# A Mamba block with a codebook FFN on one core: x dt, D x and half of the segment terms moved off GpSimd in two of its stages

## The chip, the cores and the metric

The kernel runs on one core of one Trainium2 chip. The metric is the device time of a launch in microseconds; the time before is the median of 3 runs. The engines are called PE (TensorE, matmuls), DVE (VectorE), ACT (ScalarE), POOL (GpSimd) and SP (SyncE, which here issues DMAs only).

## The reference, cut to what matters

```
x = x + layernorm(mamba(layernorm(x)))          # x: 4 x 1024 tokens of 512
x = x + layernorm(ffn(layernorm(x)))
mamba:  z, x, B, C, dt = split(u @ W_in.T)      # 512, 512, 64, 64, 8
        x, B, C = silu(conv4(x, B, C))          # causal, depthwise, 4 taps
        dt = softplus(dt + bias);  dA = exp(dt * A)          # 8 heads of 64
        S = S * dA_t + dt_t * outer(x_t, B_t)   # state 64 x 64 a head
        y = S @ C_t + D * x
        return (y * silu(z)) @ W_out.T
ffn:    w = lut[idx]                            # 16 levels, gate, up and down
        return (silu(x @ gate.T) * (x @ up.T)) @ down.T      # 512 -> 1376 -> 512
```

## The kernel before

The 4096 tokens are eight tiles of 512, a tile is four chunks of 128 tokens. A stage t runs the scan of tile t chunk by chunk, prepares tile t + 1 (projection, convolution, step sizes, z) and works on the FFN of tile t - 2 (LAG = 2). Two stages come without FFN work: tiles 0 and 1. In them the FFN weights are decoded, 20 half units a stage. For a half unit ACT turns codes into fp16 (L850), DVE makes 8 masks of 128 x 832 (L1524), PE adds them up with diagonals of the levels in two banks, 8 matmuls each (L1247), and ACT copies high and low halves out of the banks (L861, L862). Three banks turn. These stages are called decode stages here; stages 2 to 7 are FFN stages, and two tails follow.

The order of the work is written out by hand, one list an engine, with semaphores between them. A chunk c of the scan goes like this:

- POOL builds the segment terms (`segments`, L583 to L591): the causal 0/1 matrix times dt A of each of 8 heads, once for the fp16 high piece and once for the low piece, each one instruction of 128 x 1024. It may start when the inner products of the chunk before are done, since the terms lie in `decay`.
- PE turns x to token order (`prepare_x`, L1258), makes the Gram matrix of B and C and the sums (`prepare_small`), and multiplies the segment terms with a triangular matrix (`segment_sums`, L1285 to L1294), which waits for both pieces.
- ACT copies x out of its bank (L871), exponentiates the sums and the segments (`small`, `decays`); DVE multiplies by the Gram matrix (`decayed`).
- POOL (`weights`, L593 to L612) makes x dt (L598), x D (L602) and x dt times the remaining decay (L609).
- PE (`scan`, L1296 to L1314) makes the carried part of y in one bank, the inner part in another (eight fp32 products of 64 columns, L1308), and the addition to the state. POOL scales the state by its decay (L624).
- DVE (`y_sum`, `y_gated`, `y_split`) adds the two parts, updates the state (L1635), adds x D (L1640), multiplies by z and splits y into two fp16 pieces, between whose short steps it makes masks. SP transposes them by DMA for the output projection. DVE takes statistics of its result (L1663), POOL makes scale and bias of them in eight one-column instructions (L638, `out_rstd`), and ACT applies them (L895, `normalise`).

Before stage 0 the start loads and splits W_in, projects tile 0 and prepares its first chunk. There POOL makes both segment pieces of chunk 0 (L589) after the first scale of the second input pair (L580); PE waits at L1291 for them.

ACT's list in a decode stage mixes emptying decode banks (`decoded`), turning codes, the small copies above, the convolution's input, and the two normalisations; each engine's list is worked off strictly in order.

## Time and profile before

| | us |
|---|---|
| median of 3 runs (1386.94 to 1388.25) | 1387.95 |
| the profiled execution | 1389.47 |
| its span in the profile | 1387.3 |
| first scan to the last decoded unit | about 61 to 357 |

The profile is of one execution of this kernel. Its page gives busy time by engine and slice. Busy time of PE is modelled from pipelined matmuls and is no measure of how well the array is used. A wait is put down to the semaphore event that came last.

### The profile page before, as it was taken

Reading aid. Unit: us, or ns where it says so; the run is one execution under the profiler, and the core shown is the slowest. Engines: PE = TensorE matmul, PEld = TensorE weight load, DVE = VectorE, ACT = ScalarE, POOL = GpSimd, SP = SyncE. Lnnn points to the kernel's source line nnn. Section 1 sums busy time; section 2 is a strip of 40 time slices with the busy share of each in tenths; the row PEclk is TensorE's granted clock in tenths of the full one; section 3 lists DMA queues with packets and bytes.
Section 4 is the critical chain, followed back from the end, with each engine's and each line's share of the span. In section 5 each row is a group of like instructions: output and inputs, shape, how many; then the busy total and the mean of one; then the engine's idle time right before and its main releaser. Section 6 shows DMA issues by size and latency. Waiting matters only on the chain. (4 is left out here: it accounts for less than half of the span.)

```text
span 1387.3 us, 18643 instructions
## 1 busy us (share of the span) xinstructions
PE 1300.3 (94%) x6656; PEld 629.3 (45%) x6656; DVE 975.4 (70%) x1895; ACT 545.6 (39%) x986; POOL 532.6 (38%) x723
## 2 busy tenths in 40 slices
PE   4778898988899999999999999999999999999997
PEld 2334344544444444444444445444444444444443
DVE  7989988998578756875687668865886555544332
ACT  5466576756434233332334243423433223132120
POOL 1433354434434434435333534364345344400102
PEclk9899999989999999999999999999999999999999
DMA  5044235423331224023302330142213212401201
GB/s 170 25 111 112 73 98 117 113 73 78 84 54 31 69 76 84 24 54 107 84 24 61 99 92 23 34 126 62 54 31 88 51 45 45 107 31 31 77 0 53
DMA packets 132812, 96.16 MB, mean 69 GB/s; under 512 B 102000, under 2 KB 102000, under 8 KB 132720
## 3 DMA queue, kind: packets, MB, share of 16 engines
q1 hardware_dynamic: 124752, 78.74, 22.6%
q10 hardware_dynamic: 7968, 16.23, 4.4%
q8 instruction: 53, 0.87, 0.3%
q14 instruction: 39, 0.32, 0.1%
HBM read 54.05 MB, written 16.78 MB: 51 GB/s over the span
## 5 line engine op out<-in xcount | busy, mean ns | idle before, releaser
L1341 PE MATMUL bank<-fxt,ffn_hi 128*128 128x512 f16 (+1 forms) x1408 | 420.3, 380 | 10.0 <-DVE gact L1673 8.4
L1341 PE MATMUL bank<-fxt,ffn_lo 128*128 128x512 f16 (+1 forms) x704 | 267.3, 380 | 0.0
L1341 PEld LDWEIGHTS bank<-fxt,ffn_hi 128*128 128x128 f16 (+1 forms) x1408 | 139.9, 100 | 180.8 <-DVE gact L1673 11.3
L1247 PE MATMUL bank<-mask,diag 128*128 128x416 f16 x640 | 126.0, 350 | 20.0 <-ACT ffn_lo L862 11.5
L624 POOL TENSOR_TENSOR state<-state,ex 64x512 f32<-64x512 f32 x32 | 37.5, 1173 | 261.9 <-PE bank L1304 260.8
L1355 PE MATMUL bank<-ffn_hi,h_hi 128*128 128x512 f16 (+1 forms) x352 | 133.5, 379 | 0.0
L1355 PE MATMUL bank<-ffn_hi,h_lo 128*128 128x512 f16 (+1 forms) x352 | 133.3, 379 | 0.0
L1355 PE MATMUL bank<-ffn_lo,h_hi 128*128 128x512 f16 (+1 forms) x352 | 133.3, 379 | 0.0
L589 POOL TENSOR_TENSOR decay<-causal_h,da 128x1024 f16<-128x1024 f16 x64 | 122.4, 1933 | 22.1 <-PE bank L1308 17.1
L1524 DVE TENSOR_SCALAR mask<-codes_h 128x832 f16<-128x832 f16 x320 | 120.7, 436 | 5.0 <-PE bank L1247 4.6
L1673 DVE SCALAR_TENSOR_TENSOR gact<-gact,bank 128x512 f32<-128x512 f32 (+1 forms) x88 | 60.3, 685 | 86.2 <-ACT gact L901 85.3
L1552 DVE SCALAR_TENSOR_TENSOR xs<-cin,conv_w_sb,xs 128x512 f32<-128x512 f32 x114 | 108.1, 949 | 17.1 <-ACT xs L805 13.9
L901 ACT ACTIVATE gact<-bank,c_gate_half 128x512 f32<-128x512 f32 (+1 forms) x88 | 60.0, 681 | 146.7 <-PE bank L1341 144.9
L1341 PEld LDWEIGHTS bank<-fxt,ffn_lo 128*128 128x128 f16 (+1 forms) x704 | 70.7, 100 | 81.9 <-issue 0.8
L1215 PE MATMUL bank<-xt,win_hi 128*128 128x512 f16 x320 | 98.0, 389 | 4.1 <-DVE win_lo L1968 4.1
L1247 PEld LDWEIGHTS bank<-mask,diag 128*128 128x128 f16 x640 | 62.2, 101 | 86.5 <-issue 17.6
L1185 PE MATMUL bank<-win_hi,xt 128*128 128x512 f16 (+1 forms) x512 | 92.4, 275 | 3.1 <-DMA xt<-xsplit 3.1
L907 ACT ACTIVATE h_hi<-hf 128x512 f16<-128x512 f32 (+1 forms) x88 | 55.0, 625 | 83.8 <-DVE hf L1682 83.7
L1185 PE MATMUL bank<-wout_hi,yt 128*128 128x512 f16 x256 | 82.5, 384 | 5.8 <-issue 3.5
L1546 DVE TENSOR_TENSOR xsplit<-ut,xsplit 128x512 f16<-128x512 f32 x62 | 45.7, 745 | 59.8 <-ACT xsplit L776 59.6
L766 ACT ACTIVATE ut<-ut,shift,rstd 128x512 f32<-128x512 f32 x62 | 49.8, 803 | 93.1 <-POOL shift L580 92.9
L580 POOL TENSOR_TENSOR vare<-mv,eps_c 128x2 f32<-128x2 f32 x32 | 18.9, 590 | 167.4 <-DVE mv L1541 167.3
(186 smaller groups left out, 2240.5 us busy)
## 6 DMA issues: line engine op xcount, KB each, us to landing
codes_sb<-codes ACTq DMA_DIRECT2D x76, 208.0 KB, 3.5
ures<-u SPq DMA_DIRECT2D x32, 256.0 KB, 3.1
x_scratch<-x SPq DMA_DIRECT2D x32, 256.0 KB, 2.4
ut<-x_scratch SPq DMA_DIRECT2D x16, 512.0 KB, 4.3
xres<-x_scratch SPq DMA_DIRECT2D x32, 256.0 KB, 3.2
out<-dn SPq DMA_DIRECT2D x32, 256.0 KB, 2.0
ut<-u SPq DMA_DIRECT2D x15, 512.0 KB, 4.5
ffn_hi<-w_in_t SPq DMA_DIRECT2D x4, 580.0 KB, 8.6
```

The source lines that it names most:

```text
L589: seg_ready.inc(nc.gpsimd.tensor_tensor(segs[:, n], causal_h[:].unsqueeze(1).broadcast_to((P, HEADS, P)), da[:, t % HALVES, c, n, :].unsqu ...
L766: norm_steps.inc(nc.scalar.activation(buf[:, s, :], buf[:, s, :], ACT.Identity, bias=shift[:, no % 2, s:s + 1], scale=rstd[:, no % 2, s:s ...
L901: gtanh_ready.inc(nc.scalar.activation(gact[0:w, :], banks[FFN_BANKS[2 * m % 3]][0:w, :], ACT.Tanh, scale=c_gate_half[0:w, :]))
L907: hhi_ready.inc(nc.scalar.activation(h_hi[0:w, m, :], hf[0:w, :], ACT.Copy))
L1185: last = nc.tensor.matmul(out_ap, lhs, rhs, start=(k == 0), stop=(k == len(pairs) - 1))
L1215: last = nc.tensor.matmul(p.bank[:], w[:, k, cols], xt[:, :, half, k, :], start=(k == 0 and n == 0), stop=(k == KC - 1 and n == 2))
L1247: last = nc.tensor.matmul(p.bank[:, 0:COLS], diag[:, q].rearrange("p n m -> p (n m)"), mask[:, n, q, j * COLS:(j + 1) * COLS], start=(q == ...
L1341: last = nc.tensor.matmul(bank, wt[:, c0:c0 + w], fxt[:, :, half, k, :], start=(k == 0 and n == 0), stop=(k == KC - 1 and n == 2))
L1355: last = nc.tensor.matmul(banks[FFN_BANKS[turn % 3]][:], h[0:w, m, tok], wt[0:w, d0:d0 + D], start=(m == 0 and n == 0), stop=(m == MB - 1 ...
L1524: ins = nc.vector.tensor_scalar(mask[:, n, q, :], codes_h[:, count % CODE_SLOTS, :], float(2 * q), None, ALU.is_equal)
L1552: chain(conv_steps, i, CSTEPS * o + k, nc.vector.scalar_tensor_tensor(conv_sum(i, f), conv_in(i, o)[:, k:k + TILE], conv_w_sb[:, f, k:k + ...
L1673: ffn_turn.inc(nc.vector.scalar_tensor_tensor(gact[0:w, :], gact[0:w, :], 1.0, banks[FFN_BANKS[2 * m % 3]][0:w, :], ALU.add, ALU.mult))
```

## The change

In the decode stages (t < 2) alone:

- x dt is made by ACT straight out of the bank of transposed x: eight activations of 128 x 64 with dt of the head as the scale, in place of one copy (`small_x`).
- D x is made by PE: four fp32 products of x (not transposed) with diagonal matrices that hold D, 128 columns each, added up in the bank of the inner products, which follow in the same accumulation (`scan`). The four diagonals lie in the buffer `xd`; POOL builds them once, in two instructions of 64 x 512, ahead of the maximum of W_in. DVE's addition of `xd` is replaced by a semaphore increment (`y_gated`).
- The low pieces of the segment terms are made by ACT, eight scaled causal matrices of 128 x 128 a chunk (`segments_low`), with a copy of the low pieces in fp32 that DVE makes once a tile. POOL keeps the high piece.
- POOL keeps only the decay-weighted product (`weigh_x`). The lists of POOL and PE are written as a decode stage and an FFN stage each; their order is otherwise as before.

FFN stages keep the old way; the waits on `xtok_ready` and `xd_ready` count from tile 2, and the first `weights` of tile 2 waits for the last scan of tile 1 too.

```diff
 def segments(t, c):                                   # POOL
...
-    for n in range(2):
+    for n in range(1 if t < LAG else 2):
         seg_ready.inc(nc.gpsimd.tensor_tensor(segs[:, n], ...
+def weigh_x(t, c):
+    pool.wait_ge(sums_ready.sem, sums_ready.now(t, c + 1))
+    pool.wait_ge(xdt_ready.sem, xdt_ready.now(t, c + 1))
+    xw_ready.inc(nc.gpsimd.tensor_tensor(xtok, xdt, ex[:, 1, :] ..., ALU.mult))
 def weights(t, c):
-    pool.wait_ge(xtok_ready.sem, xtok_ready.now(t, c + 1))
+    pool.wait_ge(xtok_ready.sem, xtok_ready.now(t - LAG, c + 1))
+    if t == LAG and c == 0:
+        pool.wait_ge(y_done.sem, y_done.now(t - 1, SUB))
...
+pool.wait_ge(s_small, 64)                             # POOL, start
+for b in range(2):
+    rows = slice(b * NST, (b + 1) * NST)
+    nc.gpsimd.tensor_tensor(d_diag[rows], ident ..., d_sb ..., ALU.mult).then_inc(s_ddiag, 1)
+pool.wait_ge(s_ddiag, 2)
...
 def small_x(t, c):                                    # ACT
     act.wait_ge(xtok_done.sem, xtok_done.now(t, c + 1))
+    if t < LAG:
+        if t == 0 and c == 0:
+            act.wait_ge(dt_steps.sem, dt_steps.now(t, 21))
+        else:
+            act.wait_ge(y_done.sem, y_done.now(t, c))
+            act.wait_ge(xw_ready.sem, xw_ready.now(t, c))
+            if c == 0:
+                act.wait_ge(dt_steps.sem, dt_steps.now(t, 21))
+        for n in range(HEADS):
+            last = nc.scalar.activation(xdt[:, n * HD:(n + 1) * HD], tok_bank[:, n * HD:(n + 1) * HD],
+                                        ACT.Identity, scale=dt4[:, t % HALVES, c, n:n + 1])
+        xdt_ready.inc(last)
+        return
+def segments_low(t, c):
+    if t > 0 or c > 0:
+        act.wait_ge(y_done.sem, y_done.now(t, c))
+    if c == 0:
+        act.wait_ge(s_da_low, t + 1)
+    for n in range(HEADS):
+        last = nc.scalar.activation(segs[:, 1, n, :], causal_h[:], ACT.Identity,
+                                    scale=da_low[:, t, c, n:n + 1])
+    seg_ready.inc(last)
...
 def decode_stage(t):                                  # ACT
+    segments_low(t, 1)
     decoded(t, 0)
...
+    segments_low(t, 2)
     decoded(t, 5)
...
+    segments_low(t, 3)
     decoded(t, 10)
...
+    if t + 1 < LAG:
+        segments_low(t + 1, 0)
     decoded(t, 15)
...
     conv_input(0, 3)                                  # ACT, start
+    segments_low(0, 0)
     codes_to_half(0)
...
 def scan(t, c):                                       # PE
     yi_done.inc(nc.tensor.matmul(carried_bank[:], cs[h, tok], state[h, :], start=True, stop=True))
+    if dec:
+        if t == 0 and c == 0:
+            pe.wait_ge(s_ddiag, 2)
+        for k in range(KC):
+            nc.tensor.matmul(inner_bank[:, k * P:(k + 1) * P], xs[:, half, k, tok], d_diag[:, k, :],
+                             start=(k == 0), stop=False)
...
-                                xdt[:, n * HD:(n + 1) * HD], start=True, stop=True)
+                                xdt[:, n * HD:(n + 1) * HD], start=not dec, stop=not dec or n == HEADS - 1)
...
     dt_steps.inc(nc.vector.tensor_scalar(dt4[:, p], dt[:], 0.25, None, ALU.mult))   # DVE
+    if i < LAG:
+        nc.vector.tensor_copy(da_low[:, i], da[:, p, :, 1, :]).then_inc(s_da_low, 1)
...
 def y_gated(t, c):
-    dve.wait_ge(xd_ready.sem, xd_ready.now(t, c + 1))
-    y_step(t, c, 3, nc.vector.tensor_tensor(y[:], y[:], xd[:], ALU.add))
+    if t < LAG:
+        dve.sem_inc(y_steps.sem, 1)
+    else:
+        dve.wait_ge(xd_ready.sem, xd_ready.now(t - LAG, c + 1))
+        y_step(t, c, 3, nc.vector.tensor_tensor(y[:], y[:], xd[:], ALU.add))
```

## Rows read from the trace of the kernel before

**Rows 1.** The page's slices: busy tenths of PE, DVE in 40 slices.
```profile
PE   4778898988899999999999999999999999999997
DVE  7989988998578756875687668865886555544332
```

**Rows 2.** Busy time by stretch, then granted clock, DMA share, GB/s.
```profile
61.00:357.00 296.00, 253.20 (x1371) 129.10 (x1369) 258.84 (x577) 187.98 (x342) 122.69 (x139) 0.94 0.39 97
500.00:1387.00 887.00, 873.85 (x4378) 417.16 (x4375) 560.01 (x1027) 274.22 (x496) 329.92 (x457) 1.00 0.23 59
```

**Rows 3.** Waits of PE, 61 to 357 us: total, times, longest.
```profile
PE bank L1266 <- DVE state L1635: 12.2, 3, 6.4
PE bank L1247 <- ACT ffn_lo L862: 11.5, 10, 3.7
PE bank L1247 <- DVE mask L1524: 8.5, 8, 3.9
PE bank L1185 <- issue: 3.5, 1, 3.5
PE bank L1185 <- DMA xt<-xsplit: 3.1, 1, 3.1
PE bank L1185 <- DMA yt<-ysplit: 2.3, 1, 2.3
```

**Rows 4.** Waits of ACT, 61 to 357 us.
```profile
ACT x L895 <- POOL obias L638: 27.6, 4, 9.2
```

**Rows 5.** Groups of POOL, 61 to 357: count, busy us, mean ns, idle.
```profile
L589 POOL TENSOR_TENSOR decay<-causal_h,da 128x1024 f16<-128x1024 f16 x16 | 31.6, 1993 | 4.0 <-PE bank L1308 3.6 <-POOL state L624 0.2
L598 POOL TENSOR_TENSOR xdt<-xtok,dt 128x512 f32<-128x512 f32 x9 | 11.9, 1325 | 13.6 <-ACT xtok L871 13.6
L602 POOL TENSOR_TENSOR xd<-xtok,d_sb 128x512 f32<-128x512 f32 x9 | 11.7, 1298 | 0.0
```

**Rows 6.** Groups of DVE, 61 to 357 us.
```profile
L1524 DVE TENSOR_SCALAR mask<-codes_h 128x832 f16<-128x832 f16 x320 | 120.7, 436 | 5.0 <-PE bank L1247 4.6
L1640 DVE TENSOR_TENSOR y<-y,xd 128x512 f32<-128x512 f32 x8 | 9.1, 1132 | 0.0
```

**Rows 7.** Two DVE lines, whole span: duration ns min/median/max.
```profile
L1524 DVE TENSOR_SCALAR mask<-codes_h x320: 355/368/2062, 61.6 to 343.6; 128x832 f16<-128x832 f16 x160
L1640 DVE TENSOR_TENSOR y<-y,xd x32: 657/679/2265, 73.6 to 1185.2; 128x512 f32<-128x512 f32 x32
```

**Rows 8.** DVE in order of time: start us, us, what.
```profile
68.46 5.19 DVE L1524 TENSOR_SCALAR mask<-codes_h 128x832 f16<-128x832 f16 x8
95.68 2.38 DVE L1524 TENSOR_SCALAR mask<-codes_h 128x832 f16<-128x832 f16 x8
```

**Rows 9.** POOL in order of time, beside the first of them.
```profile
67.83 3.88 POOL L589 TENSOR_TENSOR decay<-causal_h,da 128x1024 f16<-128x1024 f16 x2
```

**Rows 10.** ACT in order of time, at the start.
```profile
29.35 0.27 ACT L818 ACTIVATE dtr<-bank,c_in 128x32 f32<-128x32 f32 x1
29.52 0.19 ACT L795 ACTIVATE cin<-zero_c 128x3 f32<-128x3 f32 x1
46.10 0.97 ACT L850 ACTIVATE codes_h<-codes_sb,pair_bias 128x832 f16<-128x832 int32 x1
46.98 0.61 ACT L813 ACTIVATE cin<-xs 128x512 f32<-128x512 f32 x1
```

**Rows 11.** Group of ACT, 61 to 357 us.
```profile
L871 ACT ACTIVATE xtok<-bank 128x512 f32<-128x512 f32 x9 | 5.3, 590 | 3.4 <-PE bank L1266 2.6 <-issue 0.5 <-ACT codes_h L850 0.2
```

**Rows 12.** PE in order of time, idle time before it in brackets.
```profile
55.36 1.89 PE L1291 MATMUL bank<-decay,below_h 128*128 128x512 f16 x4 [7.60 <-POOL decay L589]
100.36 2.00 PE L1308 MATMUL bank<-xdt,decay 128*128 128x64 f32 x16
116.00 0.48 PE L1276 MATMUL bank<-cs,bs 64*128 64x128 f32 x2
116.33 0.22 PE L1277 MATMUL bank<-ident,bs 64*128 64x64 f32 x1
```

More of the change, by code:

```diff
@@ L607, in weights @@
                     pool.wait_ge(xdt_ready.sem, xdt_ready.now(t, c + 1))
-                    pool.wait_ge(xd_ready.sem, xd_ready.now(t, c + 1))
+                    pool.wait_ge(xd_ready.sem, xd_ready.now(t - LAG, c + 1))
                     xw_ready.inc(nc.gpsimd.tensor_tensor(
@@ L654, in add_output, with decode_stage @@
                     res_ready.inc(nc.gpsimd.tensor_tensor(dn[:, c % 2, :], dn[:, c % 2, :], xres[:], ALU.add))
+                def decode_stage(t):
+                    decay_state(t, 0)
+                    segments(t, 1)
+                    if t >= 1:
+                        out_rstd(t - 1, 3)
+                        add_residual(t - 1, 3)
+                    weigh_x(t, 1)
+                    pair_rstd("u", t + 1, 1)
+                    decay_state(t, 1)
+                    segments(t, 2)
+                    out_rstd(t, 0)
+                    add_residual(t, 0)
+                    weigh_x(t, 2)
+                    if t >= 1:
+                        pair_rstd("x", t - 1, 0)
+                    decay_state(t, 2)
+                    segments(t, 3)
+                    out_rstd(t, 1)
+                    add_residual(t, 1)
+                    weigh_x(t, 3)
+                    decay_state(t, 3)
+                    segments(t + 1, 0)
+                    out_rstd(t, 2)
+                    add_residual(t, 2)
+                    if t + 1 < LAG:
+                        weigh_x(t + 1, 0)
+                    else:
+                        weights(t + 1, 0)
+                    if t >= 1:
+                        pair_rstd("x", t - 1, 1)
+                    pair_rstd("u", t + 2, 0)
                 def stage(t):
@@ L751, in _ @@
                 segments(0, 0)
-                weights(0, 0)
-                for t in range(TILES):
+                weigh_x(0, 0)
+                for t in range(LAG):
+                    decode_stage(t)
+                for t in range(LAG, TILES):
                     stage(t)
@@ L1357, in down, with decode_stage @@
                     down_done.inc(last)
+                def decode_stage(t):
+                    scan(t, 0)
+                    decode(t, 0)
+                    prepare(t, 1)
+                    segment_sums(t, 1)
+                    decode(t, 1)
+                    decode(t, 2)
+                    if t > 0:
+                        project_out(t, 0)
+                    decode(t, 3)
+                    decode(t, 4)
+                    if t == 0:
+                        project_out(t, 0)
+                    scan(t, 1)
+                    decode(t, 5)
+                    project_dt(t + 1)
+                    project_conv(t + 1, 4)
+                    prepare(t, 2)
+                    segment_sums(t, 2)
+                    decode(t, 6)
+                    project_conv(t + 1, 0)
+                    decode(t, 7)
+                    project_out(t, 1)
+                    decode(t, 8)
+                    decode(t, 9)
+                    scan(t, 2)
+                    decode(t, 10)
+                    project_conv(t + 1, 1)
+                    prepare(t, 3)
+                    segment_sums(t, 3)
+                    decode(t, 11)
+                    project_conv(t + 1, 2)
+                    project_conv(t + 1, 3)
+                    decode(t, 12)
+                    project_out(t, 2)
+                    decode(t, 13)
+                    decode(t, 14)
+                    scan(t, 3)
+                    decode(t, 15)
+                    project_z(t + 1, 0)
+                    prepare(t + 1, 0)
+                    segment_sums(t + 1, 0)
+                    decode(t, 16)
+                    decode(t, 17)
+                    project_z(t + 1, 1)
+                    project_out(t, 3)
+                    decode(t, 18)
+                    project_z(t + 1, 2)
+                    project_z(t + 1, 3)
+                    decode(t, 19)
@@ L1386, in stage @@
-                    if ffn:
-                        gate_up(g, 4)
+                    gate_up(g, 2)
+                    gate_up(g, 3)
+                    project_out(t, 0)
+                    gate_up(g, 4)
                     scan(t, 1)
-                    if dec:
-                        decode(t, 5)
                     if nxt:
@@ L1451, in stage @@
                         segment_sums(t + 1, 0)
[L1452 to L1457 removed]
+                    down(g, 2)
                     if nxt:
@@ L1460, in stage @@
                     project_out(t, 3)
-                    if dec:
-                        decode(t, 18)
-                    if ffn:
-                        down(g, 3)
+                    down(g, 3)
                     if nxt:
@@ L1467, in stage @@
                         project_z(t + 1, 3)
-                    if dec:
-                        decode(t, 19)
                 def tail(t):
@@ L1497, in _ @@
                 prepare_x(0, 0)
-                for t in range(TILES):
+                for t in range(LAG):
+                    decode_stage(t)
+                for t in range(LAG, TILES):
                     stage(t)
```

119 lines of the change are left out of this document (38 added, 81 removed).

## The prediction

> **What bounds the kernel now.** I read the page's slices first. They are not alike: from the eleventh slice on TensorE (PE) stands at nine tenths, before it at seven to nine, and in those same early slices VectorE (DVE) stands at eight or nine and later at five to eight [rows 1]. The table of stretches shows it in microseconds: from 500 us on PE is busy 874 of 887 us, while from 61 to 357 us, the two decode stages, it is busy 253 of 296 and DVE 259 of 296, at a mean granted clock of 0.94, so part of PE's 253 ran at the lower of the two levels (1.2 against 2.4 GHz) [rows 2]. So the FFN stages are bound by PE and the decode stages by DVE together with short round trips. The change touches the decode stages and the start only; the FFN stages I leave as they are.
>
> The waits of PE in 61 to 357 us say whom it waited for [rows 3]. On DVE end: the state update 12.2, the masks 8.5, the transposed y (which DVE splits) 2.3, the transposed input (DVE's split feeds that DMA too) 3.1, and 3.5 shown as issue; that last one stands at the first output projection of tile 0, whose wait in the code is for the low half of W_out, a DVE instruction in the queue behind the masks, so I count it with DVE. Together 29.6 us. On ScalarE (ACT) freeing a decode bank: 11.5 us. ACT itself sat 27.6 us in front of the output normalisation for eight small POOL instructions, which in turn follow DVE's statistics [rows 4]: most of ACT's idle time is DVE's lateness handed on.
>
> **Removed from POOL.** Per chunk of 128 tokens one of two segment products, the x times dt product and the D times x product. There are 8 chunks in the decode stages (the ninth instance in the window is tile 2's first chunk and stays): 8 x 1.99 = 15.9, 8 x 1.33 = 10.6 and 8 x 1.30 = 10.4 us, together 36.9 us [rows 5]. POOL has no share in the chain here, except through what it does to DVE.
>
> **Removed from DVE, directly.** y + xd, 8 times. Its median is 679 ns, its mean in the decode stages 1132 [rows 6, 7]. Undisturbed work: 8 x 0.68 = 5.4 us.
>
> **Removed from DVE, indirectly.** DVE slows while POOL works. Eight masks take 2.38 us in a quiet stretch and 5.19 us where the two segment products of 3.88 us lie beside them [rows 8, 9]: 2.81 us lost on 3.88, or 0.72 us for each us of POOL. That ratio is the upper end: 0.72 x 36.9 = 27 us. The lower end takes the masks alone: mean 436 ns against a median of 368 over 320 instructions is 22 us lost to all POOL work of the window, 122.7 us, or 0.18 per us, so 7 us [rows 2, 6, 7]. But masks are less than half of DVE's time, other two-input instructions show the same (y + xd gains 0.45 us each by this), and the three products removed are the long ones with large operands, whereas much of POOL's other time is one-column arithmetic. So I take a value near the upper row, 22 us, of which 3.6 belongs to y + xd itself. DVE falls by 5.4 + 22 = 27 us, with ends 12 and 32.
>
> A rule of the Trainium skill bears on this. "SBUF — State Buffer", section "Who interferes with whom", says that the two engines share one port pair as an exclusive lock: a VectorE instruction in a two-port mode or with two SBUF inputs and a reading GpSimd instruction do not share, one blocks wholly until the other ends. By that rule DVE would get back up to the whole length of each product beside which it has such work, up to 37 us; the trace has 0.72 on one overlap, with the direction of blocking decided by who came first. This is the larger-gain rival below. The same section says that ACT never waits for anyone, which no row here contradicts, so work moved to ACT should not be paid by DVE a second time.
>
> **Added to ACT.** Per chunk 16 small activations in place of one copy. Issue pace rather than duration counts. A 32-column one with a scale pointer from PSUM is followed by the next after 0.17 us; one of 832 columns after 0.88 us, though the duration is 0.97 [rows 10]. That is (0.88 - 0.17)/800 = 0.89 ns a column. So 128 columns: 0.17 + 96 x 0.00089 = 0.26 us, eight of them 2.0; 64 columns: 0.20 us, eight of them 1.6; less the copy of 0.59 [rows 11]. Net 3.0 us a chunk, 24 us in all, with ends 17 (the pace 0.17 for all sixteen) and 38 (durations instead of paces: 0.27 for 32 columns, so 0.30 and 0.36). ACT rises from 188 to 212 of 296 us.
>
> "ScalarE: Activation LUTs", section "Rules for kernel authors", in the Trainium skill, advises VectorE rather than ScalarE for a multiplication and budgets about 0.3 us an activation plus 0.83 ns an element. By that, called an estimate, the sixteen would cost 3.3 + 2.8 us, less the copy 5.5 a chunk and 44 in all; that rule is the one that speaks against this change.
>
> What of the 24 us lies on the path: the segment products stand where ACT otherwise waits for PE, just after the scan, before the first decoded half unit of the chunk is full (the state product and the eight matmuls of its first bank stand before that). ACT would be late there by perhaps 1 us. The x products stand in a stretch in which ACT empties banks while PE decodes, and delay each following bank by 1.0 us. PE has three banks and waited for ACT 11.5 us already. I put 2/3 us a chunk on PE's path, 5 us. Below lies 0 (hidden behind the waits of rows 4), above the whole 24.
>
> **Added to PE.** Four fp32 products of 128 columns a chunk, before the inner products. Nearest rows: one fp32 product of 128 columns stands as a pair (x2), 0.48 us with its tail, and by the starts the next instruction follows after 0.33 us; eight products of 64 columns (x16) 2.00 us, 0.25 each [rows 12]. So 4 x 0.25 = 1.0 to 4 x 0.33 = 1.3 a chunk, 8 to 10.5 us in all. The accumulation into the same bank changes nothing in the count of the inner products. They lie after the carried product and ahead of the waits for x dt and the decayed Gram matrix; PE waits for neither to speak of, so nothing hides them but PE's own idle time behind it. Where DVE sets the pace they are free, where PE does they cost in full. I take 8 us of 9.
>
> **Waits added.** ACT's segment products wait for the previous inner products, behind which PE must go anyway before it fills the next decode bank: no new lateness. The x products wait for POOL's weighing of the chunk before, long done. POOL's first full product for tile 2 waits for the last scan of tile 1, and stands behind the segments that wait for it already: nothing. DVE's replaced step is one semaphore increment. SP's queue keeps its order; its transposes come as DVE's splits do.
>
> **The start.** PE waited 7.60 us for the second segment product of chunk 0 [rows 12]; it now comes from ACT, whose input stands ready earlier, so PE goes on after one product instead of two: -1.95 us. x times dt by ACT is 1.6 us where copy and POOL product took 0.6 + 1.3 [rows 5, 11]: nearly even. The slow DVE work beside it gains about 0.5 more. The two new POOL products that build the diagonals fall into POOL's wait for the maximum of W_in; beside them DVE runs its reductions, and I put 0.5 us loss there. Sum -2.0, ends -4 and +1.
>
> **The sum in the decode stages.** Of PE's 29.6 us that end on DVE I let 22 go: DVE is 27 us lighter, but some waits then end on ACT or on DMA instead. With PE denser the clock drops less: 0.06 of 296 us is 18 us of lower granted clock, of which I take 3. So -22 - 3 + 8 + 5 = -12. The other account, from DVE: -27, less what DVE now waits more for ACT, PE and the code loads, gives -17 where the increase in waiting is 10. I take the middle, -14.5.
>
> With the start: -16.5. The profiled execution took 1389.47 us (span 1387.3); 1389.5 - 16.5 = 1373.0. The median is 1.5 us below that execution: 1371.5.
>
> **Rivals.**
> - *Larger gain.* DVE gets back almost all of the POOL time and PE follows: -28 to -32 from DVE. PE's own work is the floor: at the higher clock level and without a gap it would be 253 - 18 + 9 = 244 us against 296, so there is room. Gives about -28 with the start, 1360. For it: the 0.72 ratio, and that delays are passed round by ACT and POOL chains. Against it: ACT is then the next late one. Chance 0.16.
> - *Gain spent.* PE's 10 us and ACT's waits of 10 to 12 eat it; DVE's relief falls on stretches where it then waits for PE. Gives about -3, 1385. For it: DVE already waited for PE in places. Chance 0.14.
> - *Slower: ACT becomes the bound.* Place: the decode banks after a chunk's small copies. There ACT is already late: PE waited 11.5 us for it though ACT was busy only 188 of 296, so in a row of half units what ACT loses PE loses too. Price: the 38 us of the upper account in full, + 8 of PE, less everything that DVE held up (29.6, clock 3, start 2): +11, 1399. It decides from the point where a small activation costs its full duration and ACT's waits for the normalisation stay as long as now. The ScalarE page's budget of the Trainium skill would make it +17. Against it: 108 us of ACT idle time in the window, and those waits shrink with DVE. Chance 0.06.
> - *Forecast*, chance 0.64, its own spread 1364 to 1380.
>
> About 0.2%, 2.8 us, is what this measurement can tell from no change. Slower is the last rival's 0.06; half of "gain spent" lies within 0.2%, less what of it is beyond: 0.05; the rest 0.89 is faster. The range for 8 in 10 takes in part of the first rival and of the second: 1359 to 1382.
>
> **What would show it.** In the changed profile: the decode stages end near 340 instead of 357 us. The mask group keeps its count, with mean near 400 ns. DVE's busy time from the first scan to the end of decoding is 225 to 237 us. POOL's segment product occurs 8 times there. ACT's new groups show durations of about 0.30 and 0.36 us. PE's waits on DVE in the stretch are under 10 us, on ACT 12 to 18. PE's wait at the first segment sums is under 6 us. I would be wrong if masks kept their mean (the slowing comes then from the POOL work that stays), if PE's waits on ACT rose beyond 25 us, or if the time from 357 us on changed by more than 2 us.

## The result, and the profile after

| | before | after |
|---|---|---|
| median, 7 runs each on one chip | 1387.72 us (1386.68 to 1389.46) | 1382.71 us (1376.33 to 1383.88) |
| ratio, 95% interval | | 0.9946 (0.9931 to 0.9962) |
| profiled execution, its span | 1389.47, 1387.3 | 1382.02, 1380.3 |
| start: span's begin to the first scan | 61.9 | 66.7 |
| first scan to the ninth (the decode stages) | 291.6 | 279.1 |
| from there to the end | 1033.8 | 1034.5 |

The kernel is faster, as forecast, by 5 us between the medians and 7.5 us by the ratio (5.3 to 9.6), where 16.5 was forecast; 1382.71 lies just above the range, 1359 to 1382. The last three rows say where. I cut both spans at the carried product (PE's product of `state` and `cs`, L1304 before, L1390 after) of tile 0's first chunk, and at that of tile 2's, the ninth chunk. The decode stages got 12.5 us shorter, of 14.5 forecast. The start *grew* by 4.8 where it should have shrunk by 2.0. The spans differ by 7.0 where 16.5 was forecast; of the 9.5 us between, 6.8 are the start's, 2.0 the decode stages' and 0.7 lie behind them.

The two stretches as the view of stretches has them, first after (start, decode stages), then before, cut at the same points. Columns: length; busy us of PE, PEld, DVE, ACT, POOL with their instructions; granted clock; DMA share; GB/s.
```profile
0.00:66.70 66.70, 34.81 (x206) 17.16 (x206) 51.58 (x104) 34.93 (x61) 15.73 (x37) 0.95 0.29 89
66.70:345.80 279.10, 252.79 (x1409) 133.38 (x1408) 231.40 (x568) 212.42 (x452) 83.36 (x116) 0.95 0.41 101
```
```profile
0.00:61.90 61.90, 34.83 (x205) 17.11 (x205) 52.35 (x105) 32.45 (x53) 15.40 (x36) 0.92 0.31 96
61.90:353.50 291.60, 248.80 (x1346) 126.22 (x1345) 257.62 (x574) 186.96 (x340) 122.69 (x139) 0.94 0.39 97
```

In the decode stages DVE fell by 26.2 us, ACT rose by 25.5, POOL fell by 39.3, and PE rose by 4.0 though it got 9.3 us more work (below), at a granted clock that is 0.01 higher. The page's slices answer [rows 1]: PE's first one fell from 4 to 2 (the start), its fourth and fifth rose from 8 to 9, and of DVE's first ten three are 9 where five were. (On rows 1 the prediction says that PE stands at nine tenths from the eleventh slice; it is from the twelfth.)
```profile
PE   2879998988899999999999999999999999999997
DVE  6978977897678657875687558765886565544342
```

PE's waits in the decode stages, and ACT's largest, to be held against [rows 3, 4] (total, times, longest):
```profile
PE bank L1351 <- DVE state L1731: 9.0, 3, 4.0
PE bank L1332 <- ACT ffn_lo L917: 7.4, 4, 4.2
PE bank L1376 <- ACT decay L955: 3.5, 1, 3.5
PE bank L1270 <- issue: 2.8, 1, 2.8
PE bank L1332 <- DVE mask L1618: 1.8, 3, 1.1
PE bank L1270 <- DMA xt<-xsplit: 1.8, 1, 1.8
ACT x L974 <- POOL obias L656: 21.4, 4, 7.5
```
And the groups that the change touches, against [rows 5, 6] (count, busy us, mean ns, idle before it):
```profile
L1618 DVE TENSOR_SCALAR mask<-codes_h 128x832 f16<-128x832 f16 x320 | 109.5, 402 | 6.5 <-PE bank L1332 6.0
L596 POOL TENSOR_TENSOR decay<-causal_h,da 128x1024 f16<-128x1024 f16 x9 | 17.3, 1927 | 9.1 <-PE bank L1400 7.8 <-issue 1.1
L955 ACT ACTIVATE decay<-causal_h,da_low 128x128 f16<-128x128 f16 x56 | 17.1, 388 | 2.9 <-PE bank L1400 1.8 <-ACT codes_h L905 1.0
L935 ACT ACTIVATE xdt<-bank,dt 128x64 f32<-128x64 f32 x64 | 13.9, 324 | 2.4 <-PE bank L1351 2.2
L1395 PE MATMUL bank<-xd,xs 128*128 128x128 f32 x64 | 9.3, 288 | 0.0
```

The masks' mean went from 436 to 402 ns, POOL makes its segment product nine times in the stretch (seven, and both pieces of tile 2's first chunk; I had said 8) where there were sixteen, and the state wait fell from 12.2 to 9.0. One row is new: PE waited once, 3.5 us, for L955, the low segment pieces that the change gives to ACT.

### The profile page after: what moved, and what is told of

It is laid out like the page before. It is cut to its first block and busy times, and to the rows that moved or that the text cites. A ratio compares the mean times of both kernels' runs of the same rounds, so it can differ in the third digit from the quotient of the medians.

```text
span 1380.3 us, 18867 instructions
## 1 busy us (share of the span) xinstructions
PE 1305.2 (95%) x6720; PEld 636.7 (46%) x6720; DVE 949.3 (69%) x1889; ACT 573.5 (42%) x1106; POOL 494.7 (36%) x701
## 5 line engine op out<-in xcount | busy, mean ns | idle before, releaser
L1773 DVE SCALAR_TENSOR_TENSOR gact<-gact,bank 128x512 f32<-128x512 f32 (+1 forms) x88 | 60.2, 685 | 87.1 <-ACT gact L980 86.2
L1646 DVE SCALAR_TENSOR_TENSOR xs<-cin,conv_w_sb,xs 128x512 f32<-128x512 f32 x114 | 104.9, 920 | 19.9 <-ACT xs L860 16.8
L596 POOL TENSOR_TENSOR decay<-causal_h,da 128x1024 f16<-128x1024 f16 x56 | 105.8, 1908 | 27.2 <-PE bank L1400 21.3
L1618 DVE TENSOR_SCALAR mask<-codes_h 128x832 f16<-128x832 f16 x320 | 109.5, 402 | 6.5 <-PE bank L1332 6.0
L1332 PEld LDWEIGHTS bank<-mask,diag 128*128 128x128 f16 x640 | 62.6, 100 | 72.4 <-issue 14.4
L1640 DVE TENSOR_TENSOR xsplit<-ut,xsplit 128x512 f16<-128x512 f32 x62 | 43.5, 709 | 60.9 <-ACT xsplit L831 60.6
L1782 DVE SCALAR_TENSOR_TENSOR hf<-gact,bank 128x512 f32<-128x512 f32 (+1 forms) x88 | 60.3, 686 | 28.7 <-PE bank L1433 21.8
```

What stands on the lines that cost most here:

```text
L596: seg_ready.inc(nc.gpsimd.tensor_tensor(segs[:, n], causal_h[:].unsqueeze(1).broadcast_to((P, HEADS, P)), da[:, t % HALVES, c, n, :].unsqu ...
L1332: last = nc.tensor.matmul(p.bank[:, 0:COLS], diag[:, q].rearrange("p n m -> p (n m)"), mask[:, n, q, j * COLS:(j + 1) * COLS], start=(q == ...
L1618: ins = nc.vector.tensor_scalar(mask[:, n, q, :], codes_h[:, count % CODE_SLOTS, :], float(2 * q), None, ALU.is_equal)
L1646: chain(conv_steps, i, CSTEPS * o + k, nc.vector.scalar_tensor_tensor(conv_sum(i, f), conv_in(i, o)[:, k:k + TILE], conv_w_sb[:, f, k:k + ...
L1773: ffn_turn.inc(nc.vector.scalar_tensor_tensor(gact[0:w, :], gact[0:w, :], 1.0, banks[FFN_BANKS[2 * m % 3]][0:w, :], ALU.add, ALU.mult))
L1782: ffn_turn.inc(nc.vector.scalar_tensor_tensor(hf[0:w, :], gact[0:w, :], HSCALE, banks[FFN_BANKS[(2 * m + 1) % 3]][0:w, :], ALU.mult, ALU.m ...
```

## Where the start lost its gain

POOL in order of time, after (start, duration, what, idle time before it and what ended it):
```profile
17.61 2.72 POOL L789 TENSOR_TENSOR xd<-ident,d_sb 64x512 f32<-64x512 f32 x2 [5.84 <-DMA conv_w_sb<-conv_w]
26.04 0.38 POOL L795 PARTITION_ALL_REDUCE big<-lowest  x1 [5.71 <-issue]
36.88 0.35 POOL L797 PARTITION_ALL_REDUCE big<-lowest  x1 [10.46 <-DVE lowest L2121]
44.13 2.43 POOL L799 TENSOR_TENSOR diag<-fold,lut_sel 128x1024 f16<-128x1024 f32 x1 [6.90 <-issue]
```
The same two instructions of before, the first all-reduce and the first product behind the second:
```profile
18.60 0.38 POOL L742 PARTITION_ALL_REDUCE big<-lowest  x1 [6.81 <-DVE lowest L2004]
37.46 2.38 POOL L746 TENSOR_TENSOR diag<-fold,lut_sel 128x1024 f16<-128x1024 f32 x1 [7.47 <-issue]
```
The first all-reduce forms the maximum of W_in over partitions. Its input `lowest` is ready at 18.35 us in both kernels (DVE's reduction at 18.20 lasts 0.15). Before, it ran at 18.60. After, POOL's two diagonal products run from 17.61 to 20.33, and the all-reduce follows at **26.04**, not at 20.4: 5.71 us of "issue", in which POOL waited for nothing that is shown. The all-reduce's line in the view of one line, the sequencer's row of it, tells what lies in between. The last two times are those of its first and last occurrence. After, and then before:
```profile
L795 POOLq MODIFY_POOL_CONFIG  x2: 7/7/7, 20.3 to 20.3; - x2
```
```profile
L742 POOLq MODIFY_POOL_CONFIG  x2: 7/7/7, 11.7 to 11.8; - x2
```
A reconfiguration is put ahead of the all-reduce; I call it and what follows it a turn. Before, POOL had nothing to do from 11.79 us on, so it came at 11.8, and the 6.81 us of idle time that the row puts down to DVE's `lowest` hid it. Now it can only come behind the products, at 20.3, and is paid in full. A price for such a turn was in the trace of before: it stands on the way back from the second all-reduce to the next product, 7.47 us of "issue" (6.90 after), which I read past. There too the sequencer reconfigures, right behind the all-reduce (before):
```profile
L746 POOLq MODIFY_POOL_CONFIG  x2: 83/83/83, 29.9 to 30.0; - x2
```

The Trainium skill has the rule, "GPSIMD Engine Reference", section "2.1 Instruction dispatch": the first call to a freshly loaded kernel pays a load of about 6 us (5.95 measured, between MODIFY_POOL_CONFIG and the first instruction behind it, less the wait for events), without an instruction in the profile. The 5.71 us here agree, and the prediction did not weigh it. No run here shows what the engine does in that time.

PE's first projection and its first segment sums, after; then the first projection before:
```profile
30.78 1.01 PE L1300 MATMUL bank<-xt,win_hi 128*128 128x512 f16 x2 [11.34 <-DVE win_lo L2068]
60.47 1.04 PE L1376 MATMUL bank<-decay,below_h 128*128 128x512 f16 x2 [5.17 <-POOL decay L596]
```
```profile
23.54 1.01 PE L1215 MATMUL bank<-xt,win_hi 128*128 128x512 f16 x2 [4.07 <-DVE win_lo L1968]
```
W_in's scale hangs on the maximum, so PE starts 7.2 us later (30.78 against 23.54). Of these the start keeps 4.8; PE's wait at the segment sums fell from 7.60 [rows 12] to 5.17 us, 2.4 less, which is the gain that the prediction had seen there (1.95).

## The experiments

The ratios are against the kernel before, which ran beside each group of kernels (medians there 1387.76 to 1390.17), five rounds each; the row of before is that of the change's own comparison. "First scan" and "stretch" are cut as above, from the profiled executions; busy times are those of the stretch.

| kernel | median | ratio (95%) | first scan | stretch | DVE / ACT / POOL busy |
|---|---|---|---|---|---|
| before | 1387.72 | 1 | 61.9 | 291.6 | 257.6 / 187.0 / 122.7 |
| the change | 1382.71 | 0.9946 (0.9931 to 0.9962) | 66.7 | 279.1 | 231.4 / 212.4 / 83.4 |
| e1_diag_late | 1376.80 | 0.9914 (0.9891 to 0.9937) | 61.6 | 279.9 | 229.6 / 212.2 / 84.7 |
| e2_d_own_sem | 1376.50 | 0.9908 (0.9885 to 0.9930) | 62.4 | 277.6 | 230.2 / 212.9 / 81.2 |
| e3_before_diag_early | 1396.89 | 1.0051 (1.0035 to 1.0067) | 68.9 | 294.3 | 259.4 / 187.3 / 122.5 |
| e4_late_swap | 1377.42 | 0.9913 (0.9897 to 0.9929) | 61.8 | 282.2 | 230.6 / 212.9 / 86.8 |
| p4_d_only | 1381.67 | 0.9956 (0.9942 to 0.9971) | 64.2 | 283.3 | 246.8 / 187.1 / 106.9 |
| p1_no_seg | 1380.16 | 0.9939 (0.9917 to 0.9961) | 64.5 | 280.3 | 240.3 / 196.0 / 95.2 |
| p3_no_xdt | 1375.35 | 0.9900 (0.9882 to 0.9918) | 61.4 | 280.0 | 240.4 / 204.1 / 95.2 |
| c_no_d_pe | 1373.73 | 0.9878 (0.9856 to 0.9899) | 59.7 | 280.4 | 233.0 / 211.9 / 87.1 |
| c_pool_more | 1383.11 | 0.9957 (0.9941 to 0.9972) | 62.7 | 286.8 | 241.1 / 212.5 / 96.4 |
| c_act_twice | 1378.34 | 0.9935 (0.9914 to 0.9956) | 61.6 | 284.1 | 232.8 / 229.2 / 82.3 |
| **e5_diag_act** | **1372.68** | **0.9896 (0.9873 to 0.9918)** | 60.9 | 277.4 | 230.7 / 212.3 / 81.4 |
| b1_diag_act_no_xdt | 1375.66 | 0.9913 (0.9899 to 0.9927) | 59.4 | 282.7 | 239.4 / 203.6 / 93.9 |

First scan and stretch are of one execution each, so their spread matters. Five kernels share the change's decode stages (the change, e1, e2, e4, e5). Their stretches are 277.4 to 282.2 us; in them PE is busy for 250.8 to 254.9 us, at granted clocks of 0.94 to 0.96, and idle for 26.3 to 29.0. The kernel before and e3 share theirs: 291.6 and 294.3. c_no_d_pe has e1's code up to the first scan and comes to it at 59.7, e1 at 61.6. So under 5 us between two stretches, or 2 us between two first scans, can be no more than this spread.

### The start: e1, e2, e3, e4

**e1_diag_late** moves the diagonals behind both all-reduces.
```diff
-pool.wait_ge(s_small, 64); <two products>; pool.wait_ge(s_ddiag, 2)
 pool.wait_ge(s_lowest, 1)
 nc.gpsimd.partition_all_reduce(big[:, 0:1], lowest[:, 0:1], ...)
 pool.wait_ge(s_wbig, 1)
 nc.gpsimd.partition_all_reduce(big[:, 1:2], lowest[:, 1:2], ...)
+pool.wait_ge(s_wall, 1); <two products>; pool.wait_ge(s_ddiag, 2)
```


> The changed kernel with the two products that build the D diagonals moved behind POOL's two all-reduces, with a wait for the second of them. Theory A (turning POOL from elementwise products to an all-reduce costs it about 5.7 us after the last product, which the kernel before hid in its wait for the maximum of W_in and the changed kernel does not): the first all-reduce is back from 26.0 us to about 18.6, the first scan from 66.7 to about 59.3, and the time falls by 7.4 us from 1382.7 to about 1375.3. Theory B (only the lateness of the products themselves counts, 20.3 us against the 18.4 at which the maximum is ready, and the gap behind them is something of that execution): 1.9 us, about 1380.8.

**e2_d_own_sem** leaves them early but lets them wait for the load of D alone; the shared semaphore also waits for `conv_w`, which lands last.
```diff
-pool.wait_ge(s_small, 64)
+pool.wait_ge(s_dload, 16)
```


> The changed kernel with the diagonals where it has them, but waiting for the transfer of D alone (landed at 12.1 us) and not for all four small ones (the convolution weights land at 17.5). Theory A: products from 12.1 to about 14.5 us, the turn of 5.7 us until 20.3, so the first all-reduce at about 20.3 instead of 26.0: 5.7 us better than the changed kernel, about 1377.0, and 1.7 us behind the kernel with the diagonals late. Theory B: the all-reduce at 18.6, the same time as with the diagonals late.

**e3_before_diag_early** is the kernel before with the two products put in the same place, their result unused.
```diff
+pool.wait_ge(s_small, 64); <two products>; pool.wait_ge(s_ddiag, 2)
 pool.wait_ge(s_lowest, 1)
```


> The kernel before with the two products that build the diagonals added at the place the change gives them, with its wait; nothing uses them. Theory A: first all-reduce at 26.0 us, the time rises by 7.4 us from 1387.7 to about 1395.1, which is the whole of what the change lost at the start. Theory B: by 1.9 us, about 1389.6.

POOL of e1 and, behind it, DVE of e1; then POOL of e2; then POOL and PE of e3:
```profile
18.52 0.38 POOL L787 PARTITION_ALL_REDUCE big<-lowest  x1 [6.81 <-DVE lowest L2105]
37.05 2.83 POOL L794 TENSOR_TENSOR xd<-ident,d_sb 64x512 f32<-64x512 f32 x2 [7.15 <-issue]
37.56 1.42 DVE L1661 SCALAR_TENSOR_TENSOR cs<-cin,x 64x512 f32<-64x512 f32 x1
39.01 1.42 DVE L1656 SCALAR_TENSOR_TENSOR xs<-cin,xs 128x512 f32<-128x512 f32 x1
40.36 1.91 DVE L1676 TENSOR_SCALAR dtp<-dte 128x32 f32<-128x32 f32 x1
```
```profile
12.17 2.49 POOL L790 TENSOR_TENSOR xd<-ident,d_sb 64x512 f32<-64x512 f32 x2 [0.41 <-DMA d_sb<-d_param]
20.21 0.38 POOL L796 PARTITION_ALL_REDUCE big<-lowest  x1 [5.55 <-issue]
```
```profile
17.60 2.67 POOL L747 TENSOR_TENSOR xd<-ident,d_sb 64x512 f32<-64x512 f32 x2 [5.91 <-DMA conv_w_sb<-conv_w]
25.90 0.38 POOL L753 PARTITION_ALL_REDUCE big<-lowest  x1 [5.63 <-issue]
30.65 0.58 PE L1226 MATMUL bank<-xt,win_hi 128*128 128x512 f16 x1 [11.27 <-DVE win_lo L1979]
```

The reduction comes where the turn puts it: at 18.52 with no product ahead of it; at 20.21 where the products end at 14.66, that is 5.55 behind them; at 25.90 where they end at 20.27 (5.63 behind). In e3 nothing else is changed, and the kernel before gets 7.1 us slower by the ratio (4.9 to 9.3), its first scan comes 7.0 later, and PE's first projection stands at 30.65 as it does in the changed kernel. Seen against e3, the changed kernel's first scan is 2.2 us earlier: the gain of 2.0 that I had worked out for the start exists, under a cost of 7. So the turn behind the early products is shown as the cause: e3 adds it alone, e2 and e1 take it away. The rival that the expectations set against it, that only the 1.9 us count by which the products end too late, falls by e3, and by e2, where they end long before the maximum is ready. (By the ratios e2's interval lies clear of the change's; e1's overlaps it by a little.)

The recovery in e1 is 5.1 us of first scan against the changed kernel, and not the 7.4 expected. A part of the rest is seen: the products now lie at 37.05 to 39.88 beside DVE's convolution, whose two rows of e1 took 1.42 us each, where the kernel before has 0.69. The 1.91 us of the third row are not theirs; it took as long before, beside the level table's product alone:
```profile
37.97 1.91 DVE L1581 TENSOR_SCALAR dtp<-dte 128x32 f32<-128x32 f32 x1
```
DVE's step sizes, which the segment products need, come later by this, and PE's wait there is 6.74 us in e1 (5.17 in the changed kernel):
```profile
55.54 1.89 PE L1377 MATMUL bank<-decay,below_h 128*128 128x512 f16 x4 [6.74 <-POOL decay L596]
```

**e4_late_swap** is e1 with POOL's segment product of chunk 0 ahead of its scales for the second input pair.
```diff
-pair_rstd("u", 1, 0)
 segments(0, 0)
+pair_rstd("u", 1, 0)
```


> The kernel with the diagonals late, and POOL's high segment product of chunk 0 ahead of the scale of the second tile's first pair, for which PE had waited 5.2 us. By the timeline of the changed kernel, less 7.4 us, PE's wait at the first segment sums falls from 5.2 to about 1 us; but the x of chunk 0 is complete on DVE only 1.2 to 2.8 us before PE wants it now, so the first scan comes 1 to 3 us earlier: 1372 to 1374.5. If that wait is worth its whole length, 1371; if DVE sets the first scan, 1375.3 as without the swap.

PE in order of time:
```profile
51.20 1.04 PE L1377 MATMUL bank<-decay,below_h 128*128 128x512 f16 x4 [1.80 <-ACT decay L956]
60.76 1.12 PE L1352 MATMUL bank<-ident,xs 128*128 128x128 f32 x4 [3.34 <-DVE xs L1656]
```
PE's wait at the segment sums, 6.74 in e1, went down to 1.80, and the first scan did not move (61.8 against 61.6), where 1 to 3 us were expected: PE only waits 3.34 us later for DVE's convolution of x. That is the next late thing at the start; I had gone by the longest wait. (In this run alone the all-reduce came 7.87 us after the reconfiguration, at 19.61, which is 1.1 later than in e1 and can hide as much of a gain. I can't say why.)

### The parts: p4, p1, p3

All three are e1 with a part given back to POOL. **p4_d_only** gives back both x dt and the low segment pieces, so only D x on PE is left of the change; **p1_no_seg** gives back the segment pieces, **p3_no_xdt** x dt.
```diff
 def segments(t, c):                                # p1, p4
-    for n in range(1 if t < LAG else 2):
+    for n in range(2):
 def weigh_x(t, c):                                 # p3, p4
+    pool.wait_ge(xtok_ready.sem, xtok_ready.now(t, c + 1))
+    xdt_ready.inc(nc.gpsimd.tensor_tensor(xdt, xtok, dt4[...], ALU.mult))
```


> Of the change only the D products on PE (diagonals late), with x dt and both segment pieces on POOL as before. Theory C (moving the low pieces and x dt to ACT brings nothing between the scans, since each alone undone left the stretch at 280 us): stretch 279 to 282 us against 291.6 of the kernel before, first scan at about 64.5, ratio 0.992 to 0.994; the D part, 5.4 us of DVE and 10 of POOL, is then the whole gain of 12. Theory D (the two parts stand in for each other: each alone relieves POOL enough, both undone don't): stretch 285 to 289, ratio 0.996 to 0.999.

> The kernel with the diagonals late, and both segment products on POOL again (x dt stays on ACT, D x on PE). Base: 0.9914 of the kernel before, 279.9 us from the first to the ninth scan. Port theory (what counts is that POOL's long products slow DVE): 16 us of POOL come back, DVE loses some 0.6 of it, 10 us, of which half to two thirds show: the stretch is 5 to 7 us longer, the start 2 us more, ratio about 0.997. ACT theory (ACT's 19 us for the low pieces cost as much as POOL's relief brings): stretch the same or shorter, ratio 0.989 to 0.992.

> The kernel with the diagonals late, and x dt on POOL again from ACT's one copy (low segment pieces stay on ACT, D x on PE). Port theory: 10.6 us of POOL come back, DVE loses about 6, 3 to 4 show, less the 8 us of ACT time saved, of which 1 to 2 show: stretch 1 to 3 us longer, ratio 0.9925 to 0.994. ACT theory: the x products lie where ACT is late for PE's banks, so the stretch is 2 us or more shorter, ratio under 0.991.

The stretch of p4_d_only, and of e1 for comparison (columns as above):
```profile
64.20:347.50 283.30, 252.22 (x1409) 133.48 (x1408) 246.75 (x567) 187.11 (x340) 106.89 (x131) 0.96 0.39 100
```
```profile
61.60:341.50 279.90, 250.90 (x1409) 133.67 (x1408) 229.58 (x568) 212.21 (x452) 84.72 (x116) 0.95 0.39 101
```
D x on PE alone brings 8.3 of the 11.7 us that the stretch of e1 gains. The 25.1 us of work moved to ACT bring the other 3.4 (1.1 to 5.9 against the five stretches above), though they free DVE of 17.2 us. DVE's relief in the two steps is 10.8 and 17.2 us, and even at the ends of that spread the time follows the first far better than the second. p4's 283.3 and its ratio lie between the ranges of the two theories; by the ratios it is 5.8 us slower than e1, the intervals apart, of which 2.6 are the first scan's. Given back alone, either of ACT's parts changes the stretch by less than 0.5 us, with 11 us more on DVE and 8 to 16 less on ACT: neither of the theories set against each other for p1 and p3 came out whole. A gain from x dt on ACT is not seen: p3 is at 0.9900 against e1's 0.9914, the intervals overlap. The segment pieces seem to bring something at the start: without them the first scan comes 2.9 us later (64.5; 64.2 in p4), where both pieces of chunk 0 are POOL's again. The ratio of p1 overlaps with e1's.

Where ACT's side is paid shows in DVE's wait for `gram`, which ACT copies out behind the new activations. After the change, then p3, then p1:
```profile
DVE gram L1705 <- ACT gram L946: 7.9, 6, 3.8
```
```profile
DVE gram L1701 <- ACT gram L942: 1.8, 2, 0.9
```
```profile
DVE gram L1700 <- ACT gram L947: 5.5, 5, 2.1
```
It was 1.3 us before. In all three kernels without x dt on ACT (p3, p4, b1) it is 1.8; in e1, from which p1 and p3 are made, it is 8.1.

### The sizes: c_no_d_pe, c_pool_more, c_act_twice

**c_no_d_pe** leaves D x out of the decode stages altogether (part of the computation is missing), to price PE's products.
```diff
-for k in range(KC):
-    nc.tensor.matmul(inner_bank[:, k * P:(k + 1) * P], xs[...], d_diag[:, k, :], ...)
```


> The kernel with the diagonals late, without PE's D products in the decode stages: D x is left out there, so its time is that of the work without it. Eight times four products take 9.3 us of PE in the changed kernel's profile. If PE sets the pace of the decode stages now, as the prediction's term of 8 us has it: stretch 8 us shorter, ratio about 0.9855. If DVE still sets it most of the time: 0 to 3 us, ratio 0.989 to 0.9914.

By the medians they cost about 3 us of their 9.3, by the ratios 5, and the intervals overlap; the profiled stretch is not shorter at all (280.4 against 279.9), and that execution was the slowest of its kernel. Both values lie below the 8 that I charged, but the intervals leave anything from about 1 to 9, so this does not settle it.

**c_pool_more** makes the high segment piece twice on POOL, seven more products; **c_act_twice** makes the low pieces twice on ACT.
```diff
+nc.gpsimd.tensor_tensor(segs[:, 0], causal_h ..., da ..., ALU.mult).then_inc(s_extra, 1)
+pool.wait_ge(s_extra, t * SUB + c + 1)
```
```diff
-for n in range(HEADS):
+for twice in range(2): for n in range(HEADS):
     nc.scalar.activation(segs[:, 1, n, :], causal_h[:], ACT.Identity, scale=da_low[...])
```


> The kernel with the diagonals late, and in the decode stages POOL makes the high segment piece twice, the second time over the first. No other engine's work changes; the terms come 2 us later. Port theory: POOL has 15.5 us more of the kind that was taken away; masks and two-input instructions of DVE lengthen by about 10 us in sum, the stretch by 5 to 7 us plus 2 us at the start, ratio 0.9965 to 0.998. If POOL's time does not matter to DVE's pace: only the start's 2 us, ratio about 0.993.

> The kernel with the diagonals late, and ACT makes the eight low segment pieces twice, the second time over the first: 19.5 us more of ACT in eight places, nothing else changed. The prediction's term (24 us of ACT work put 5 on the path) gives +4 in the stretch and +2 at the start, ratio about 0.996. By the pair of kernels measured since (POOL's 15.5 us more cost 6.9 in the stretch, and the same with ACT's 19 us taken off cost 0.4), ACT's load is worth 6 to 7 in the stretch, ratio 0.997 to 0.999. If ACT's pieces are hidden in its wait for PE, stretch unchanged.

The stretch of each, with the wait of PE that grew:
```profile
62.70:349.50 286.80, 252.24 (x1410) 133.59 (x1409) 241.06 (x568) 212.47 (x452) 96.39 (x123) 0.95 0.40 98
PE bank L1358 <- DVE state L1738: 12.3, 3, 5.5
```
```profile
61.60:345.70 284.10, 254.16 (x1410) 134.19 (x1409) 232.83 (x569) 229.17 (x508) 82.28 (x116) 0.94 0.40 99
PE bank L1382 <- ACT decay L958: 5.6, 1, 5.6
```
13.5 us of POOL products (7 of 1923 ns) made DVE 11.5 us busier, 0.85 for each us, and the stretch 6.9 us longer, with PE idle for 34.6 us in place of 29.0. PE's wait for DVE's state update is 12.3; it is 8.2 to 9.1 in the five kernels above. By the ratios c_pool_more is 6.0 us slower than e1, the intervals apart. So POOL's products reach the time through DVE, with about 0.6 us of stretch for each us of DVE.

c_act_twice says less. 17.0 us of ACT came with a stretch 4.2 us longer, but PE's idle time grew by 0.9 of it only (29.0 to 29.9): its wait at the segment sums went from 3.1 to 5.6, and its wait for ACT's decode banks fell from 12.4 to 9.6. The other 3.3 us are PE's busy time, 254.2 against 250.9, for the same matmuls at a granted clock of 0.94 against 0.95; e4, with e1's decode stages, has 254.9 at 0.94. By the ratios it is 2.9 us slower than e1 and the intervals overlap. ACT's extra work costs at most about 0.25 for each us here; that it costs anything is not shown.

### A better version: e5, b1

**e5_diag_act** lets ACT build the diagonals, in eight activations, where it waits for PE's first projection; **b1_diag_act_no_xdt** adds p3's edit.
```diff
-pool.wait_ge(s_small, 64); <two products>; pool.wait_ge(s_ddiag, 2)          # POOL
+for k in range(KC):                                                         # ACT
+    for b in range(2):
+        nc.scalar.activation(d_diag[rows, k, :], ident[rows, :], ACT.Identity,
+                             scale=d_sb[rows, 2 * k + b:2 * k + b + 1]).then_inc(s_ddiag, 1)
```


> The kernel with the diagonals late, but built by ACT in eight small activations in its idle time before the first convolution input (2.6 us of wait there in the kernel before), and by POOL not at all. What is told apart is why the start is no better than before though POOL's all-reduce is at its old place: if it is the two POOL products at 37 us, which hold up DVE, the first scan comes at about 59.3 instead of 61.6 and the ratio is about 0.990; if it is something else, 61.6 stays and with it 0.991.

> D x on PE, low segment pieces and diagonals on ACT, x dt on POOL as before: the candidate for the fastest. x dt back on POOL measured 0.990 with the diagonals on POOL; with the start 2.3 us shorter about 0.9884. If the start does not shorten, 0.990.

ACT of e5, then DVE's three instructions at the place where e1's were slow, then its stretch:
```profile
25.14 3.36 ACT L1214 ACTIVATE xd<-ident,d_sb 64x128 f32<-64x128 f32 x8
37.83 2.31 DVE L1657 SCALAR_TENSOR_TENSOR cs<-cin,x 64x512 f32<-64x512 f32 x1
40.17 0.69 DVE L1652 SCALAR_TENSOR_TENSOR xs<-cin,xs 128x512 f32<-128x512 f32 x1
40.78 0.17 DVE L1672 TENSOR_SCALAR dtp<-dte 128x32 f32<-128x32 f32 x1
60.90:338.30 277.40, 250.77 (x1409) 133.45 (x1408) 230.67 (x567) 212.33 (x452) 81.37 (x116) 0.96 0.40 102
```
The eight activations fill ACT's wait for PE from 25.14 to 28.5 us. DVE's rows take 2.31, 0.69 and 0.17 us, 3.2 in sum where e1 has 4.8 and the kernel before 3.3: the level table's product on POOL still lies beside one of them, here the first. PE's wait at the segment sums is back at the changed kernel's value:
```profile
54.22 1.89 PE L1373 MATMUL bank<-decay,below_h 128*128 128x512 f16 x4 [5.17 <-POOL decay L596]
```
They start 1.3 us earlier than in e1, the first scan only 0.7 (60.9, where 59.3 was expected if the products were the whole reason). In both kernels PE's f16 products of 512 columns go from 0.63 to 0.38 us at about 60.0 us, so e5 does more of them in the slow stretch. e5 is the fastest kernel that keeps the whole computation, 1372.68 us: 15.1 below the kernel before by the medians, 14.4 by the ratio (11.4 to 17.6), and by the ratios 7 below the change. Against e1 and e2 its interval overlaps, and what of its lead is real isn't settled. Giving x dt back to POOL here (b1) did not show the gain expected (0.9913 where 0.9884 was): the first scan is at 59.4, the stretch 5.3 longer, and its interval overlaps with e5's.

## Why the prediction was wrong

**The failed step is the start.** The prediction put it so: "The two new POOL products that build the diagonals fall into POOL's wait for the maximum of W_in; beside them DVE runs its reductions, and I put 0.5 us loss there." With "Sum -2.0, ends -4 and +1" for the whole start. Measured: +4.8. What failed is that this wait was not empty. It held the turn to the all-reduce, which takes 5.55 to 5.71 us behind the last element-wise product. I had also placed the products too early: they waited for the shared semaphore of four small loads, the last of which landed at 17.5, where D was there at 12.1, so they ended at 20.33, 2 us past the moment at which the reduction's input was ready, and the turn came on top. e3 shows the step by itself at +7.0 for the first scan. The 0.5 for DVE was short too: two of its rows there take 0.95 and 0.90 us (0.23 and 0.24 before), 1.4 lost, in time in which the all-reduce was late anyway.

The other steps, by their own terms:

- *DVE lighter by 27 (ends 12 and 32).* 26.2. The value near the upper row was the right one: 20.8 of it is indirect, 0.56 for each of the 36.9 us of POOL products, and c_pool_more has 0.85 for the products that stay beside masks.
- *ACT heavier by 24 (17 to 38).* 25.5. ACT's row of eight 128-column activations takes 2.43 us (e1 at 47.13), 0.30 each; I had 0.26. The durations forecast, 0.30 and 0.36, measured 0.324 and 0.388. The budget of "ScalarE: Activation LUTs", section "Rules for kernel authors", in the Trainium skill gave 44; the measurement decides against it for activations in a row.
- *ACT's share on the path, 5 of 24.* Not confirmed: c_act_twice allows up to 0.25 for each us, so up to 6 of 25, and does not show that it is more than nothing. But "no new lateness" of the segment pieces was wrong: PE's 3.5 us for them at chunk 1 are new, and so is most of DVE's 7.9 for `gram`.
- *PE's products, 8 of 9.* 9.3 us of work for 32 products; PE's busy time rose by 4.0. c_no_d_pe puts 3 to 5 on the path, with an interval that takes in 8.
- *PE's waits on DVE.* Under 10 was forecast, from 29.6; by the same count (state, masks, the issue row, the input's and y's DMA) it is 15.4. The wait on ACT's banks is 7.4, with the new one 10.9, where 12 to 18 was forecast. In e1, e2, e4 and e5, with the same decode stages, the two waits on ACT come to between 12 and 15.5, so 10.9 is one execution's value and the forecast was about right.
- *The sum from PE, -12.* It came out at -12.5, near by luck: DVE gave back 14.2 of the 22 I let go, ACT's waits fell by 0.6 where I added 5, and two waits for POOL (1.6 us) went, which I hadn't counted. The errors cancel. The forecast missed by 2.0 because I took the middle of this sum and the next one.
- *The sum from DVE, -27 and 10 more of waiting.* DVE's idle time in the stretch went from 34.0 to 47.7, by 13.7. With 26.2 for 27 that makes -12.5 in place of -17.
- *The clock.* 0.94 to 0.95, as far as I had it.
- *The FFN stages unchanged.* 1033.8 and 1034.5.
- *The decode stages end near 340 instead of 357.* ACT's last copy out of a bank starts at 346.4 us, at 354.1 before: 7.7 earlier, the two misses together.

The rivals: *gain spent* was nearest in time, and its mechanism isn't what happened, since the decode stages kept 12.5 of 14.5. *Larger gain* did not come though DVE got nearly all back: at 279 us the stretch is far from PE's 253, and DVE now waits more for ACT (`xsplit` 12.6, `gram` 7.9; 11.6 and 1.3 before). *ACT becomes the bound* did not come.

What stays open: why executions of the changed kernel spread over 7.5 us, from 1376.33 to 1383.88, where those before spread over 2.8 beside it. Beside the other kernels the one before spread over 4.9 to 6.7 (11 or 12 executions each), so this need not be the change's doing. And whether x dt on ACT helps or not lies within the intervals.

## What to carry to other kernels

Idle time in front of an instruction is free only if the waiting engine had nothing to prepare in it: where GpSimd's all-reduce follows element-wise products, look for the sequencer's reconfiguration and count a turn before the gap is filled. A stall shown as "issue" elsewhere in the same trace prices it. And when three parts of a change free one engine, price the last one against the engine that takes the work: here the first 10.8 us of DVE relief brought 8.3 us, and the next 17.2, paid with 25 us on ACT, 3.4.

## What the runs showed of the hardware

- GpSimd's turn from element-wise products to the all-reduce took 5.71, 5.55 and 5.63 us (the changed kernel, e2, e3) from the end of the last product; e4 has 7.87 after a reconfiguration made while the engine idled, unexplained. The way back to a product took 6.8 to 7.5 us in all kernels. Both directions pay. Where the engine had nothing to do the reconfiguration came at 11.8 us, ahead of an all-reduce at 18.6 (before).
- A GpSimd product beside VectorE's work slows short one-input instructions too: a 128x32 one of 0.17 us (e5) took 1.91 (e1, L1676) and ended at 42.27, when the product beside it did (42.23).
- Eight activations of 64x128 fp32 take 3.36 us in a row, 0.42 each, where eight of 128x128 fp16 take 2.43, 0.30 each. They differ in type, in partitions, and in that each of the first increments a semaphore; the three weren't told apart.
